# Perceiver kernel: context rows laid 13 to a partition, and a busy TensorE with an earlier weight product at the start

## The reference, cut to what matters

```python
x = x + xattn(layernorm(x), ctx, ctx, Wq, bq, Wk, bk, Wv, bv)    # x (16, 64, 256), ctx (16, 1601, 256)
# xattn, one head:  q = x @ Wq + bq,  k = ctx @ Wk + bk,  v = ctx @ Wv + bv
#                   softmax(q @ k.T / sqrt(256)) @ v
x = x + selective_scan_layer(layernorm(x), ...)
x = x + spiking_ffn(layernorm(x), ...)
x = x + windowed_xattn(layernorm(x), ctx, ...)
x = x + phase_attention(layernorm(x), ...)
x = x + top2_experts(layernorm(x), ...)
```

## Time and profile before

| | us |
|---|---|
| median of 3 runs | 678.44 (677.01 to 678.97) |
| the profiled execution, its own time | 678.84 |
| span of that execution, first to last instruction | 677.1 |
| of it setup and cross attention | about 161 |
| TensorE busy in the whole span | 606.3 |

### The profile page before, as it was taken

How to read it: one execution, slowest core, us unless ns; L and a number is a source line. 1 busy time by engine, 2 the same in 40 slices (tenths; PEclk the granted TensorE clock), 3 DMA queues, 4 the chain that set the end, 5 groups by cost and what they waited for, 6 DMA issues and landing times. The chain is left out here.

```text
span 677.1 us, 11619 instructions
## 1 busy us (share of the span) xinstructions
PE 606.3 (90%) x4390; PEld 459.3 (68%) x4390; DVE 471.5 (70%) x793; ACT 367.8 (54%) x692; POOL 229.6 (34%) x182
## 2 busy tenths in 40 slices
PE   4999998899995677878878999999999999999997
PEld 4455544454354666767767888887787767889897
DVE  3733333346856999999999546678978768876554
ACT  1411111125768799999999543433566456556342
POOL 2000000000029799999989300033652020231000
PEclk9999999999997799999999999999999979999999
DMA  8999999994902122233331000000100022110000
GB/s 314 398 395 394 389 389 390 395 324 138 269 6 94 62 95 94 94 109 110 105 106 40 1 1 1 16 1 18 35 3 2 1 63 78 51 60 1 32 1 31
DMA packets 31294, 86.47 MB, mean 128 GB/s; under 512 B 8076, under 2 KB 19816, under 8 KB 29064
## 3 DMA queue, kind: packets, MB, share of 16 engines
q1 hardware_dynamic: 31096, 85.67, 35.3%
q10 hardware_dynamic: 144, 0.06, 0.1%
HBM read 83.50 MB, written 1.11 MB: 125 GB/s over the span
## 5 line engine op out<-in xcount | busy, mean ns | idle before, releaser
L764 POOL TENSOR_TENSOR dbu<-du,bs 128x1024 f32<-128x1024 f32 x63 | 149.2, 2396 | 11.6 <-DVE w_in L1010 8.2
L889 ACT ACTIVATE weighed<-T,CT 128x256 f32<-128x256 f32 x222 | 94.1, 575 | 8.2 <-PE T L1089 7.8
L1010 DVE TENSOR_TENSOR_SCAN w_in<-hS,dbu 128x1024 f32<-128x1024 f32 x42 | 94.7, 2273 | 2.2 <-POOL dbu L764 1.7
L878 ACT ACTIVATE hS<-delta,negA 128x504 f32<-128x504 f32 x128 | 89.6, 795 | 6.1 <-DVE w_in L1010 2.8
L1089 PE MATMUL T<-ident,w_in 128*128 128x128 f32 x336 | 47.3, 284 | 23.4 <-ACT weighed L889 13.5
L1103 PE MATMUL Y<-ident,weighed 128*128 128x128 f32 x512 | 67.7, 275 | 0.1
L1089 PEld LDWEIGHTS T<-ident,w_in 128*128 128x128 f32 x336 | 37.3, 143 | 34.1 <-DVE w_in L1010 28.7
L1103 PEld LDWEIGHTS Y<-ident,weighed 128*128 128x128 f32 x512 | 58.7, 142 | 0.8 <-DVE sres L1031 0.3
L297 PE MATMUL O<-cN,pT 128*64 128x256 f32 x384 | 46.7, 385 | 6.7 <-DMA cN<-in_ctx 6.7
L1010 DVE TENSOR_TENSOR_SCAN xn<-hS,dbu 128x1024 f32<-128x1024 f32 x22 | 50.0, 2274 | 3.4 <-ACT hS L878 3.3
L383 POOL COPY w_xp<-w_xp 128x64 f32<-128x64 f32 x3 | 0.6, 236 | 146.7 <-DMA w_out<-in_w_out 146.7
(11 more groups left out here) (424 smaller groups left out, 1365.7 us busy)
## 6 DMA issues: line engine op xcount, KB each, us to landing
cT<-in_ctxT SPq DMA_DIRECT2D x8, 3202.0 KB, 22.5
cN<-in_ctx SPq DMA_DIRECT2D x8, 3072.0 KB, 25.2
bs<-b_rows SPq DMA_DIRECT2D x32, 512.0 KB, 3.6
raw_w<-in_w SPq DMA_DIRECT2D x16, 256.0 KB, 2.9
w<-in_w SPq DMA_DIRECT2D x7, 256.0 KB, 8.1
vs<-vx SPq DMA_DIRECT2D x8, 136.0 KB, 2.4
x<-in_x SPq DMA_DIRECT2D x2, 512.0 KB, 5.5
cR<-in_ctx SPq DMA_DIRECT2D x8, 128.0 KB
```

The costliest lines, as they stand in the source:

```text
L764: e.tensor_tensor(dbu[s % NB][:, :, :], half(m.du, s // DS), row, ALU.mult).then_inc(s_bu, 1)
L878: i = e.activation(by_batch(A[s % 2][:, j * HALF:(j + 1) * HALF]), by_batch(m.delta[:, c, h * HALF:(h + 1) * HALF]), ACT.Exp, scale=m.negA ...
L889: i = e.activation(weighed[s % 2][:, q * Q:(q + 1) * Q], T[:, q * Q:(q + 1) * Q], ACT.Copy, scale=c_of(s, q))
L1010: e.tensor_tensor_scan(S[s % NS], A[s % 2][:, :], dbu[s % NB][:, :, :].rearrange("p c n -> p (c n)"), 0.0, ALU.mult, ALU.add).then_inc(s_h, 1)
```

## The change

Three edits.

**Rows.** `cN` holds 13 rows to a partition: 123 partitions hold 1599 rows, and the last 2 rows of each batch go into a 124th partition. The two DMAs of `load_rest` and the tile `cR` are gone; `load_rows` is now two DMAs, into partitions 0 to 111 and 112 to 122, and `load_rest` one small one. There are still 13 transposes and 13 pairs of products for each tile, now of 124 or 123 keys. TensorE waits for all three DMAs at once, ahead of the first group.

**TensorE busy.** In the setup block TensorE makes 20 transposes of the identity as soon as that stands, and 10 more around the first step of the fold; nobody reads their results. ScalarE takes one square root in the setup.

**Order.** The product of the query and key weights comes ahead of the transposes of the first tokens; the bias products come after them. Two copies move between VectorE and ScalarE.

```diff
-ROWS = LK // P
-MAIN = ROWS * P
-REST = LK - MAIN
+ROWS = LK // P + 1
+FULL = LK // ROWS
+EVEN = FULL // 16 * 16
+REST = LK - FULL * ROWS
...
 def load_rows(e, k, i, r):
-    e.dma_start(k.cN[r][:, :, :, :], k.ctx[2 * i:2 * i + 2, 0:MAIN, :].rearrange("b (p c) d -> p b c d", c=ROWS)
+    for p in (slice(0, EVEN), slice(EVEN, FULL)):
+        e.dma_start(k.cN[r][p, :, :, :],
+                    k.ctx[2 * i:2 * i + 2, p.start * ROWS:p.stop * ROWS, :].rearrange("b (p c) d -> p b c d", c=ROWS)
+                    ).then_inc(k.s_dN[r], 16)
+
+
+def load_rest(e, k, i, r):
+
+    e.dma_start(k.cN[r][FULL:FULL + 1, :, 0:REST, :], k.ctx[2 * i:2 * i + 2, FULL * ROWS:LK, :].unsqueeze(0)
                 ).then_inc(k.s_dN[r], 16)
 
-
-def load_rest(e, k, i, r):
-
-    for rows in (slice(0, 64), slice(64, REST)):
-        e.dma_start(k.cR[r][rows, :, :], k.ctx[2 * i:2 * i + 2, MAIN + rows.start:MAIN + rows.stop, :].rearrange("b p d -> p b d")
-                    ).then_inc(k.s_dR[r], 16)
...
         def keys(c):
-            return slice(c, c + (P - 1) * ROWS + 1, ROWS) if c < ROWS else slice(MAIN, LK)
+            return slice(c, c + (n_keys(c) - 1) * ROWS + 1, ROWS)
 
         def n_keys(c):
-            return P if c < ROWS else REST
+            return FULL + 1 if c < REST else FULL
...
+            def keep_busy(n):
+
+                for i in range(n):
+                    e.transpose(X[:, i % 4 * P:(i % 4 + 1) * P], k.ident[:, :], k.ident[:, :])
...
-                if g == 3:
-                    e.wait_ge(k.s_dR[r], 32 * (i // 2 + 1))
                 for c in groups[g]:
                     for b in range(2):
-                        v = cN[r][:, b, c, :] if c < ROWS else cR[r][:, b, :]
-                        j = e.matmul(O[64 * b:64 * b + 64, 0:D], pT[0:n_keys(c), c, 64 * b:64 * b + 64], v,
-                                     start=c == 0, stop=c == ROWS)
+                        j = e.matmul(O[64 * b:64 * b + 64, 0:D], pT[0:n_keys(c), c, 64 * b:64 * b + 64],
+                                     cN[r][0:n_keys(c), b, c, :], start=c == 0, stop=c == ROWS - 1)
...
+            keep_busy(6)
+            turn_query_weights()
+            keep_busy(4)
+            fold()
             turn_first(0)
-            e.wait_ge(k.s_w0, k.n_w0)
-            fold()
+            fold_query_bias()
             project(0)
...
-                    e.wait_ge(s_dN[(i - 1) % 2], 16 * ((i - 1) // 2 + 1))
+                    e.wait_ge(s_dN[(i - 1) % 2], 48 * ((i - 1) // 2 + 1))
...
+            keep_turned()
             root_first(0)
+            keep_fold()
             move_first(0)
             move_first(1)
-            keep_fold()
+            keep_bias()
             root_first(1)
...
+            @block.tensor
+            def _(e):
+                e.wait_ge(k.s_const, 2)
+                for i in range(20):
+                    e.transpose(busy[:, i % 4 * P:(i % 4 + 1) * P], k.ident[:, :], k.ident[:, :])
...
                 e.dma_start(k.cols[:, :], t["cols"]).then_inc(k.s_w0, 16)
+                e.wait_ge(k.s_const, 2)
+                e.activation(root0[:, :], k.ident[:, 0:1], ACT.Sqrt)
```

More of the change, by code:

```diff
@@ L135, in cross_attention @@
         qbk = sb("qbk", [P, TILES])
-        cT, cN, cR, s_dT, s_dN = k.cT, k.cN, k.cR, k.s_dT, k.s_dN
+        cT, cN, s_dT, s_dN = k.cT, k.cN, k.s_dT, k.s_dN
         prob = [sb(f"prob{r}", [P, LK]) for r in range(2)]
-        pT = sb("pT", [P, ROWS + 1, P])
+        pT = sb("pT", [P, ROWS, P])
         mx = sb("mx", [P, 1])
@@ L233, in fold, with fold_query_bias @@
                 i.then_inc(s_fold, 1)
+            def fold():
+                e.wait_ge(s_fs, 1)
+                for r in range(KD):
+                    for c in range(KD):
+                        i = e.matmul(tps[0][:, r * D:(r + 1) * D], wqT[:, c, r * P:(r + 1) * P], k.wk0T[:, c, :],
+                                     start=c == 0, stop=c == 1)
+                i.then_inc(s_fold, 1)
+            def fold_query_bias():
                 for m in range(KD):
@@ L238, in fold, with fold_key_bias @@
                 i.then_inc(s_fold, 1)
+            def fold_key_bias():
                 e.wait_ge(s_fv, 1)
-                for r in range(KD):
-                    for c in range(KD):
-                        i = e.matmul(tps[0][:, r * D:(r + 1) * D], wqT[:, c, r * P:(r + 1) * P], k.wk0T[:, c, :],
-                                     start=c == 0, stop=c == 1)
-                i.then_inc(s_fold, 1)
                 for c in range(KD):
@@ L255, in project @@
                     if n == 1:
+                        fold_key_bias()
                         turn_first(1)
+                        e.wait_ge(s_fs, 3)
                     if n >= 2:
@@ L387, in _, with keep_turned, keep_bias @@
         def _(e):
+            def keep_turned():
+                e.wait_ge(s_fold, 1)
+                e.activation(wqT[:, :, 0:D], O[:, :].rearrange("p (c n) -> p c n", c=KD), ACT.Copy).then_inc(s_fs, 1)
             def keep_fold():
                 e.wait_ge(s_fold, 2)
+                e.activation(wqk[:, :, :], tps[0][:, :].rearrange("p (c n) -> p c n", c=KD), ACT.Copy).then_inc(s_fs, 1)
+            def keep_bias():
+                e.wait_ge(s_fold, 3)
                 e.activation(qcol, tps[1][:, 0:KD], ACT.Copy).then_inc(s_fs, 1)
-                e.wait_ge(s_fold, 3)
-                e.activation(wqk[:, :, :], tps[0][:, :].rearrange("p (c n) -> p c n", c=KD), ACT.Copy).then_inc(s_fs, 1)
             def move(n):
@@ L396, in move @@
                 e.wait_ge(s_pp, n + 1)
-                e.wait_ge(s_fs, 1)
+                e.wait_ge(s_fs, 3)
                 e.activation(qkT[:, m, h * HALF:(h + 1) * HALF], tps[n % 2][:, :], ACT.Identity, bias=qcol[:, m:m + 1]
@@ L3072, in perceiver @@
         k.cN = [sb1(f"cN{r}", [P, 2, ROWS, D]) for r in range(2)]
-        k.cR = [sb1(f"cR{r}", [REST, 2, D]) for r in range(2)]
-        k.s_dR = [sem(f"a_dR{r}") for r in range(2)]
         k.w_v0 = t["wv0"]
@@ L3099, in early_loads @@
             e.dma_start(k.b2[:, :], t["b2"]).then_inc(k.s_w6, 16)
-        with nc.Block() as block:
+        with ExitStack() as sctx, nc.Block() as block:
+            sb0, ps0, _ = tools(nc, sctx)
+            busy = ps0("busy")
+            root0 = sb0("root0", [P, 1])
+            @block.tensor
[3 more added lines that the diff above has]
+                    e.transpose(busy[:, i % 4 * P:(i % 4 + 1) * P], k.ident[:, :], k.ident[:, :])
             @block.sync
```

7 lines of the change are left out of this document (3 added, 4 removed).

## The result

| | kernel before | changed kernel |
|---|---|---|
| median, us | 678.39 (677.01 to 678.97, 4 runs) | 771.38 (758.07 to 779.31, 4 runs) |
| ratio of the shorter executions, 95% interval | | 1.1245 [1.1154, 1.1336] |
| the profiled execution, its span | 678.84, 677.1 | 775.16, 773.4 |
| step from v to v in cross attention | 15.05, from tile 3 on 16.8 to 17.1 | 26.3 to 33.8 |

The changed kernel is 12% slower. The forecast was 703 us, with 718 at the top of its range: the sign and the place were right, the size was between a quarter and a third of what came. The four executions of the changed kernel lie 21 us apart in a fast and a slow state, and the ratio is that of the two fast ones (767.60 and 758.07, some 84 us over the kernel before), while the profiled one, 775.16, is a slow one.

What follows compares the result with a forecast made beforehand. Context transfers on the DMA engines were taken as the bound; -1.4 + 1.6 + 3.1 = +3.3 us a tile moved v7 by 24.5, from the median 678.44 to 702.9, stated as 703 us, range 671 to 718.

Steps and rivals of the forecast that it cites:

- What bounds the kernel: Cross attention: context transfers set the pace from tile 3 to tile 6; dips, 1.1 us in the mean, are `cR`'s work.
- The law behind the dips: Context transfers into SBUF: a packet's speed hangs on how many partitions are written, about 3.3 GB/s for each.
- 112 partitions, +2.0 us: `cN` transfer into 112 partitions, each tile: loss taken as the middle of +1.0 and +3.0 us; with fewer bytes, net +1.6.
- 11 partitions, +2.4 us: Transfer into 11 partitions, each tile: 0.7 us at full rate plus a loss of 2.4, together +3.1 us.
- The sum: Cross attention: -1.4 + 1.6 + 3.1 = +3.3 us a tile on the transfer chain, moving v7 by +24.5 us.
- The old rest, -1.4 us: Removing the rest's old DMAs saves 0.3 us of bytes and 1.1 us of dip in each tile.
- The start, nothing: Setup: `scores(0)` 1 us later to 5.5 earlier than 23.07, covered by the DMA chain, so no change in time.
- "The columns, not the keys: nothing": 13th piece, 123 keys instead of 65: transposes, copies and products are paced by the columns, so no cost.
- Rival B: Partitions don't matter, dips come from the many 1 KB rows: -1.1 us a tile, 671.0 us; chance 0.28.
- C: Like for like: the 112-partition transfer loses nothing, the 11-partition one 1.1 us; 0 a tile, 678.4 us; chance 0.12.
- D: TensorE waits 4 us and more every tile and falls to 1.2 GHz, adding 2 to 4 us; no separate chance.

Runs made afterwards that it cites:

- the rows alone: The kernel before with the new rows (112 and 11 partitions, 13 rows each) and the old start: 765.58 us median, profiled execution 761.80 us.
- the serial kernel: The changed kernel with `cT` and `cN` made to wait for each other so they are never in flight together: 761.90 us, ratio 1.1236.
- 112+16: The kernel before with the 12 rows of all 128 partitions moved by two DMAs, into partitions 0 to 111 and 112 to 127: 748.20 us.
- 1 KB runs: The kernel before with its rest in one DMA into 128 partitions from a padded context, pieces still 1 KB: 673.39 us, ratio 0.9914.
- the transfers alone: No computation against any kernel: context rows moved into various partition counts, one transfer or pair after the other, `x` copied to the output: 244.25 us.

## Why the prediction was right or wrong

**What bounds the kernel**: right. The transfers lead from tile 3 on, and the dips are the 64-partition transfer's work: without it, or with it in 128 partitions or at another place, 5 to 7 us go.

**The law behind the dips**: wrong, and this is the step that failed. The prediction saw 203 to 214 GB/s into 64 partitions and 425 into 128 and made one number of them, 3.3 GB/s for each partition. Two points don't tell a line from a step. 120 partitions move 200, 64 at another place 421. Between the two points lay a factor of two, and the 64 from 32 and from 28 show it to be two engines to a port. The prediction quoted the ports with their partitions and the number of engines, but used the ports only to count how many the 11 partitions reach, and never asked how many engines stand at each.

**112 partitions, +2.0 us**: mis-sized, the first of the two terms that made the sum too small. 12.6 us for tile 0 instead of 7.0, a loss of 5.6. The bound from above was no bound: it took the 298 GB/s of a dip, but a dip is a mixture of a small slow transfer and of large ones at full rate around it. A transfer that is itself the slow one goes lower, 236. The law gives 9.0 us here (the share-out worked through block by block; seven neighbours to an engine straddle two ports), so it too is short for this count: 11 us alone (264 to 280 GB/s), 12.6 in the kernel.

**11 partitions, +2.4 us**: about right for tile 0. 82 GB/s for 4 us is a loss of some 3; the trace agrees here with the section "Door 1: The DMA port swizzle" of the Trainium skill's page "SBUF — State Buffer", quoted in the prediction, whose three ports had 82 and 3.6 us. What they cost in later tiles isn't shown: left out, they bring between 7 and 27 us in the whole, within the spread.

**The sum**: its parts stood beside each other as if they had the engines in turn. Measured by parts: `cT` 7.9, 12.6, 4, makes 24.5 a tile; the steps from v1 to v6 are 28.5 in the mean with the rows alone (761.80) and 32.1 in the changed kernel (775.16). The second missing term is what a slow transfer does to the `cT` in flight with it: 4.0 to 7.6 us a tile against the bare parts, some 6 of the engines' time against the serial kernel, and each is more than the 3.3 that the prediction had for a tile in all. It put nothing there. Added up for the changed kernel's profiled execution, v0 comes 4.2 later, the six steps to v6 take 186.5 us instead of 97.2, and v7 follows 2.7 later: +96.3 instead of +24.5.

**The old rest, -1.4 us**: right, though hidden here. In the kernel before its removal, or its move to 32, takes the step from 16.9 to 15.05, where TensorE leads.

**The start, nothing**: right. `scores(0)` came 4.5 us earlier, inside the "1 later to 5.5 earlier", and the product that took 3.65 us takes 2.00, and the kernel's time is unchanged. In the changed kernel the timeline begins so:

```profile
1.76 4.53 PE L3133 MATMUL busy<-ident 128*128 128x128 f32 x20 [1.76 <-POOL ident L3169]
6.58 1.02 PE L234 MATMUL X<-ident 128*128 128x128 f32 x6 [0.30 <-PEq L3124]
...
8.72 2.00 PE L249 MATMUL ptp<-wk0T,xn 128*128 128x256 f32 x8 [0.25 <-ACT xn L409]
```

**"The columns, not the keys: nothing"**: wrong by 1.34 us a tile where TensorE leads. It had the moving side of the transposes in mind; the keys are the columns of the weights, and 123 of them load in 339 ns. In the changed kernel it is hidden behind the transfers. Nowhere in the trace of before is a count near that, so it should have had bounds and not a zero.

**Rival B** fell with the 112+16 and the 1 KB runs, **C** with the transfers alone. **D** came true in the rows, PEclk 0.72 to 0.83 and 3.68 us for 1.95, but costs next to nothing: from v7 to the start of the scan layer, at 258.61, there are 14.6 us, 0.7 more than before, and from v7 to the end of the span 529.4 in both.

**A better kernel**: three kinds of variant come out at 672 to 673 us, 1% under the kernel before: the rest at partitions 32 to 95 (672.30, nothing padded), everything in 128 x 13 from a padded context (672.10), or the rest alone padded (673.39). None of them can be told from another; each interval lies clear of no change. They stop where TensorE's own 15.05 us a tile, or the plain bytes, begin to lead.

## What to carry to other kernels

Move context in one DMA over all 128 partitions, padded in DRAM if need be, and never cut off a few partitions to make the count even; where 64 are all there is, 32 to 95 ran at twice the rate of 0 to 63 here (421 against 205 GB/s). When a rate is half of another, look for two that share one thing before drawing a line through the two points, and don't take an average over a disturbed stretch for a bound on the disturber. A slow transfer's price is paid by those in flight beside it as well, so price it by rows that show it both alone and in company.

## What the runs showed of the hardware

- The cut decides a DMA's rate into this memory: 128 partitions 426 GB/s; 120, 96, 64 from 0 and 64+64 together 200 to 228; 112 alone 245 to 280, in the kernel 236; 64 from 32 at 421; 64 from 28 at 403 and then 25.
- A port's 27.2 GB/s, as the section "Door 1: The DMA port swizzle" of the Trainium skill's page "SBUF — State Buffer" has it, is near what 16, 8 and 4 partitions from 0 moved in long transfers (109, 61, 31 GB/s for four, two and one port; the last two are 12 and 14% above it). Short ones of two pieces to a partition moved up to twice that in a single microsecond (200, 106, 53); no run shows why.
- Every second partition from 32 to 94 moves 200 to 217 though by the law no two engines share a port, and every second or every fourth of all 128 moves 423 and 424 where it has 213; open.
- `cT` and the slow `cN` in flight together keep the engines busy for 28.5 us a tile, one after the other for 22.4.
- A weight load of 128 x 123 fp32 takes 339 ns, of 124 193 to 196, of 128 199 to 220, of 97 160, of 81 147.
- The eight products of the query and key weights took 2.00 us after thirty transposes of the identity and four of the weights, from 1.76 on; in the kernel before, where TensorE begins at 9.16, the same eight took 3.65. PEclk shows 1.00 in both, so the row of the granted clock doesn't show this difference.
